# Weights in the program's layout, transposes inside the first product halves, and another order of the first queries

## The chip, the cores and the metric

One core of a Trainium2 chip runs the whole kernel. The metric is the device time of one execution in microseconds (us); lower is better. TensorE (PE) does matmuls and transposes, VectorE (DVE), ScalarE (ACT) and GpSimd (POOL) the elementwise work, SyncE (SP) and ACT issue the DMAs.

## The reference

The input is 4 sequences of 512 rows by 512 columns. The same macaron layer is applied: half a feed-forward block, an attention block, half a feed-forward block, each on a layer norm of the running sum.

```python
x = x + 0.5 * ffn(layernorm(x))       # y = x @ W_base.T + b, plus 4 gated rank-8 LoRA experts
x = x + attn(layernorm(x))            # 32 heads, latent keys and values of rank 64, causal
x = x + 0.5 * ffn(layernorm(x))       # same weights as the first

# ffn:   z = x @ A.T (4 experts x 8), alpha = softmax(log(prior) + x @ router.T + router_b)
#        y += sum_e alpha_e * 2 * z_e @ B_e.T
# attn:  c_q = x @ w_q_down (192), c_kv = x @ w_kv_down (64), k_rope = rope(x @ w_k_rope) (64)
#        q_lat = (c_q @ w_q_up_nope per head) @ w_uk per head, q_rope = rope(c_q @ w_q_up_rope)
#        probs = softmax((q_lat . c_kv + q_rope . k_rope) / sqrt(192), causal)
#        out = concat over heads((probs @ c_kv) @ w_uv.T) @ w_out
```

All is float32. The kernel splits each matmul operand into a high and a low part (names ending in `_hi` and `_lo`) and sums three products.

## The kernel before

The program is written engine by engine: every engine has its own in-order list of instructions, and semaphores tie the lists together. Nothing is planned at run time; the order in each list is the order in the code. It has these stages.

**Opening.** Weights are loaded and brought into the form that the matmuls need. `transpose_base` (L710 to L722) turns `W_base` with 16 PE transposes; `base_high` on ACT and `base_low` on DVE split the result. `transpose_lora` does the same for the small LoRA and router weights. Then the first feed-forward block runs on the 4 row tiles of sequence 0 (`s` = 4 to 7: `FIRST` is 4, `DOWN` is 8). One step of a tile on PE is: `ffn_products` half 0 (12 matmuls, 292 columns: half of the output, the LoRA `z` and the router logits), then `transpose_z` of the tile before, `transpose_x` of the tile after, `ffn_products` half 1 (12 matmuls, 256 columns), then `lora` of the tile before. Each transposed tile goes through ACT (`xT_high`) and DVE (`xT_low`) before the next products may use it. `gate_logits` and `gate_rows` on DVE, with `gate_exponentials` on ACT between, make the gated `z` (tile `za`) that `transpose_z` needs.

After that come the folds. `w_q_up_nope` is turned by `transpose_nope` (PE), copied out of PSUM by `nopeTa_copy` (ACT) and `nopeTb_copy` (DVE), and multiplied with `w_uk` in `fold_query` (8 groups of 4 heads); `query_hi` (ACT) and `query_lo` (DVE) split the product into the query weights. `fold_output` multiplies `w_uv` and `w_out` of a pair of heads (16 pairs); `output_hi` (ACT) and `output_lo` (DVE) split that. In the loop over the 8 groups, `fold_output` of group g - 1 follows `fold_query` of group g. The inputs of `fold_output` pass through 4 slots (`SLOTS_OUT`); SP refills a slot when PE has used it. The other 8 output folds lie between the down projections of the 4 row tiles (`s` = 8 to 11). The rotary query weights are split by ACT (`rotary_hi`) and POOL (three long subtractions with the down weights, L585, L589 and L592). POOL then makes the norms' rough deviations of the down tiles (`rough_deviations(2, ...)`).

`opening_queries` makes the queries of the first two heads in four parts: rows 0 to 383 of both heads (`EARLY`), then rows 384 to 511 of both (`LATE`). Each part goes PE, DVE (`q_rotary`), POOL (`q_sum`), ACT (`qT_high`), POOL (`qT_low`). The first score slot needs rows 384 to 511 of head 0.

**Attention** of a sequence: 80 slots, with scores, softmax, transposes, the product with the values, and output products, spread over all engines.

**Mixed steps**, between two attentions, three times: the second feed-forward block of sequence b (tiles 0 to 3), the first of sequence b + 1 (tiles 4 to 7) and its down projections (8 to 11), in the order 4, 5, 6, 7, 8, 0, 9, 1, 10, 11, 2, 3. On PE it is `steps` (L866); `down_products` has two halves of 6 matmuls. The norm of the next tile (`xn`) is made by ACT just ahead; for tile 8 it hangs on a chain of statistics on DVE, deviations on POOL and `norm` on ACT, and next to a down tile it is queued on ACT behind `down_copies`.

**Last steps**: the second feed-forward block of sequence 3 alone, tiles 0 to 3, and the stores.

## Time and profile before

| | us |
|---|---|
| median of 3 runs (lowest, highest) | 1167.78 (1166.98, 1170.35) |
| the profiled execution, its own time | 1167.57 |
| span of its instructions, first to last | 1165.8 |
| PE, DVE, POOL, ACT busy | 1105.7, 908.2, 740.0, 623.9 |
| opening, up to the first scores | 0 to 96.7 |
| the first mixed steps | about 319 to 370 |
| last feed-forward products to the end | 1142.8 to 1165.8 |

The profile is of one execution. Busy times are sums over an engine; matmuls overlap, so PE's busy time is an upper reading. All times below are from the start of the span. L with a number is a line of the kernel before.

### The profile page before, as it was taken

The page shows a single profiled execution, that of the slowest core. Times are in us where ns is not written, and L with a number is a line of the kernel's source. Part 1 is how long each engine was busy: PE and PEld are TensorE (multiplying, and loading weights), DVE is VectorE, ACT ScalarE, POOL GpSimd, SP SyncE. Part 2 cuts the span into 40 slices and gives each one's busy share as a digit, 9 for nine tenths or more (in the row PEclk, how much of TensorE's full clock was granted, in tenths as well). Part 3 has the DMA queues.
Part 4 walks back from the last instruction along what each step waited for, and adds up shares of the span by engine and source line. Part 5 has one row for each costly group of instructions (what it writes and reads, how often), then busy time and mean ns, then how long its engine had stood idle before and what let it go on. Part 6 is the DMA issues. An engine that isn't in the chain of part 4 may idle for free.

```text
span 1165.8 us, 21866 instructions
## 1 busy us (share of the span) xinstructions
PE 1105.7 (95%) x7284; PEld 906.6 (78%) x7284; DVE 908.2 (78%) x2667; ACT 623.9 (54%) x1733; POOL 740.0 (63%) x951
## 2 busy tenths in 40 slices
PE   5896999999998999999999899999999899999997
PEld 4755788888797788888788678888888678888876
DVE  4767888888676888878776888788867787888855
ACT  3554655555454655555535555655545466555542
POOL 2406977887432978787631887787723598877841
PEclk9998999999999999999999999999999999999998
DMA  9660000000101000000101000000010100000000
GB/s 286 179 194 1 1 1 1 1 1 1 37 10 64 2 1 2 1 1 1 37 1 37 37 2 1 2 1 2 1 37 28 47 1 1 1 1 2 1 1 37
DMA packets 22248, 30.96 MB, mean 27 GB/s; under 512 B 9302, under 2 KB 11094, under 8 KB 21498
## 3 DMA queue, kind: packets, MB, share of 16 engines
q1 hardware_dynamic: 19770, 24.85, 6.7%
q10 hardware_dynamic: 2368, 4.72, 1.2%
q8 instruction: 59, 0.97, 0.3%
q14 instruction: 51, 0.42, 0.1%
HBM read 22.23 MB, written 4.19 MB: 23 GB/s over the span
## 4 chain that ended last, share of the span: by engine, by line
PE 79%; DVE 7%; POOL 7%; ACT 3%; issue 2%; SPq 1%; DMA 1%; POOLq 0%; DVEq 0%
PE Y L983 15%; PE Y L957 12%; PE XZ L942 11%; PE Y L906 10%; PE XZ L922 6%; PE XZ L923 6%; PE XZ L921 5%; PE Y L675 4%; POOL prob L631 3%; PE XZ L675 2%; POOL qT_lo L542 2%; PE XZ L650 2%; POOL q_sums L537 2%; DVE xT_lo L1281 1%; ACT xT_hi L1037 1%
## 5 line engine op out<-in xcount | busy, mean ns | idle before, releaser
L1228 ACT ACTIVATE prob<-XZ,small 128x512 f32<-128x512 f32 (+3 forms) x512 | 266.3, 525 | 282.8 <-DVE small L1622 282.8
L631 POOL TENSOR_TENSOR prob<-prob,small 128x512 f32<-128x512 f32 (+3 forms) x512 | 360.7, 721 | 50.1 <-DVE small L1576 40.4
L1622 DVE CUSTOM_DVE_ANT_0 XZ<-XZ,mask 128x512 f32<-128x512 f32 (+3 forms) x512 | 247.9, 506 | 114.6 <-PE XZ L923 110.5
L537 POOL TENSOR_TENSOR q_sums<-q_sums,q_turned 64x512 f32<-64x512 f32 (+2 forms) x130 | 164.2, 1263 | 201.5 <-DVE q_turned L1564 200.1
L942 PE MATMUL XZ<-ident,prob 128*128 128x128 f32 x1280 | 196.3, 276 | 3.2 <-POOL prob L631 2.9
L921 PE MATMUL XZ<-kT_hi,qT_hi 128*128 128x512 f32 (+3 forms) x512 | 176.9, 345 | 12.7 <-ACT prob L1228 6.8
L542 POOL TENSOR_TENSOR qT_lo<-q_sums,qT_hi 128x512 fp32r<-128x512 f32 (+2 forms) x130 | 165.2, 1271 | 31.9 <-ACT qT_hi L1195 31.8
L942 PEld LDWEIGHTS XZ<-ident,prob 128*128 128x128 f32 x1280 | 149.5, 140 | 43.2 <-POOL prob L631 10.6
L922 PE MATMUL XZ<-kT_lo,qT_hi 128*128 128x512 f32 (+3 forms) x512 | 165.4, 323 | 0.0
L923 PE MATMUL XZ<-kT_hi,qT_lo 128*128 128x512 f32 (+3 forms) x512 | 165.2, 323 | 0.0
L957 PE MATMUL Y<-probT,ckv 128*64 128x384 f32 (+2 forms) x1280 | 152.3, 384 | 0.0
L390 ACT ACTIVATE probT<-XZ 128x512 f32<-128x512 f32 x192 | 114.9, 598 | 66.0 <-PE XZ L942 64.8
L957 PEld LDWEIGHTS Y<-probT,ckv 128*64 128x64 f32 x1280 | 81.8, 136 | 60.7 <-issue 47.3
L921 PEld LDWEIGHTS XZ<-kT_hi,qT_hi 128*128 128x128 f32 x512 | 97.2, 190 | 22.8 <-issue 7.7
L983 PE MATMUL Y<-wo_hi,oT_hi 128*128 128x512 f32 x256 | 110.9, 433 | 1.5 <-DVE x_sb L1580 1.4
L1580 DVE TENSOR_TENSOR x_sb<-Y,x_sb 128x512 f32<-128x512 f32 x128 | 87.8, 686 | 29.4 <-PE Y L983 29.1
L1228 ACT ACTIVATION_READ_ACCUMULATOR prob<-XZ,small 128x1 f32 x512 | 101.9, 199 | 0.0
L923 PEld LDWEIGHTS XZ<-kT_hi,qT_lo 128*128 128x128 f32 x512 | 97.3, 190 | 5.5
L922 PEld LDWEIGHTS XZ<-kT_lo,qT_hi 128*128 128x128 f32 x512 | 97.7, 191 | 4.8
L983 PE MATMUL Y<-wo_hi,oT_lo 128*128 128x512 f32 x256 | 101.1, 395 | 0.0
L983 PE MATMUL Y<-wo_lo,oT_hi 128*128 128x512 f32 x256 | 100.2, 391 | 0.0
L1195 ACT ACTIVATE qT_hi<-q_sums 128x512 fp32r<-128x512 f32 (+2 forms) x130 | 80.2, 617 | 19.0 <-POOL q_sums L537 19.0
(220 smaller groups left out, 2162.0 us busy)
## 6 DMA issues: line engine op xcount, KB each, us to landing
wout_nat<-in_L_attn_w_out_dram SPq DMA_DIRECT2D x16, 512.0 KB, 5.0
out_dram<-x_sb SPq DMA_DIRECT2D x16, 256.0 KB, 2.0
x_next<-_attn_hidden_states_dram SPq DMA_DIRECT2D x12, 256.0 KB, 3.4
x_sb<-x_next SPq DMA_DIRECT2D x12, 256.0 KB, 2.3
wbase_nat<-in_L_ffn_W_base_dram ACTq DMA_DIRECT2D x1, 1024.0 KB, 5.7
x_sb<-_attn_hidden_states_dram ACTq DMA_DIRECT2D x4, 256.0 KB, 7.0
nope_a<-_L_attn_w_q_up_nope_dram ACTq DMA_DIRECT2D x1, 1024.0 KB, 5.4
rope_a<-_L_attn_w_q_up_rope_dram SPq DMA_DIRECT2D x1, 1024.0 KB, 8.0
```

Of the source, the lines that this page charges most:

```text
L537: nc.gpsimd.tensor_tensor(q, q, turned, ALU.add).then_inc(q_sum_set, 1)
L542: nc.gpsimd.tensor_tensor(qT_lo[par][:, head, cols], q_sums[par][:, head, cols], f32(qT_hi[par][:, head, cols]), ALU.subtract).then_inc(qT ...
L631: last = nc.gpsimd.tensor_tensor(prob[u % RING][:, c:c + w], prob[u % RING][:, c:c + w], inv_sum[:, u % RING, m:m + 1].broadcast_to([P, w] ...
L906: last = nc.tensor.matmul(bank[:, cols], w, c, start=(j == 0), stop=(j == 4))
L921: nc.tensor.matmul(bank[:, c:c + w], high, kT_hi[:, 0:w], start=True, stop=False)
L922: nc.tensor.matmul(bank[:, c:c + w], high, kT_lo[:, 0:w], start=False, stop=False)
L923: last = nc.tensor.matmul(bank[:, c:c + w], low, kT_hi[:, 0:w], start=False, stop=True)
L942: last = nc.tensor.transpose(probT_ps[v % 2][:, at], prob[v % RING][:, at], ident[:])
L957: last = nc.tensor.matmul(o_ps[64 * h:64 * h + 64, column * P:(column + n) * P], ckv[:, j, :], probT[:, HEAD_BLOCKS * h + at:HEAD_BLOCKS * ...
L983: last = nc.tensor.matmul(bank, o[buffer][:, rows], w, start=(k == 0 and j == 0), stop=(k == 1 and j == 2))
L1228: last = nc.scalar.activation(prob[u % RING][:, c:c + w], score_ps[u % 2][:, c:c + w], ACT.Exp, bias=neg_max[:, u % RING, m:m + 1], scale= ...
L1622: last = nc.vector.tensor_tensor_reduce(bank, bank, mask[:, S - w:S], -1.0, HIGHEST, ALU.add, ALU.min, neg_max[:, u % RING, m:m + 1])
```

## The change

The host hands some weights over in another layout, so that PE need not turn `W_base` and `w_q_up_nope`, and so that the DMAs move long rows. `base_sb` is the turned base weight, in another place of SBUF, which is shared with the slots of `w_out`. ACT and DVE split it in two halves of 1024 columns, not in 8 pieces. The order of the loads on ACT's queue is now row tile 0, base weight, other row tiles, `w_uk`, first half of `w_q_up_nope`.

The eight query folds now follow each other, over four PSUM banks, and the first eight output folds follow behind them. The split of the down weights on ACT stands behind the fourth query fold. The gate's matmul (`spread_gates`) moves into the first products.

In all feed-forward and mixed steps, `transpose_z` and `transpose_x` move from the end of half 0 into its middle, and on DVE `z_low` and `xT_low` move ahead of `gate_logits`. The four query parts change order: head 0 rows 0 to 383, rows 384 to 511 of head 0 and head 1, then head 1 rows 0 to 383.

```diff
-                def ffn_products(b, s, half):
+                def ffn_products(b, s, half, inside=None):
                     a, z = ((0, W0), (W0, WB))[half]
                     for c in range(KC):
+                        if c == KC // 2 and inside:
+                            inside()
...
-                def down_products(b, s, half):
+                def down_products(b, s, half, inside=None):
                     for c in (2 * half, 2 * half + 1):
+                        if c == 1 and inside:
+                            inside()
...
+                def spread_gates():
+                    pe.wait_ge(turns_one, 1)
+                    pe.wait_ge(gate_in, 16 * 2 * NE)
+                    nc.tensor.matmul(gate_ps, cosT[0:1, 0:P], gate_row[:], start=True, stop=True).then_inc(gate_spread, 1)
...
                 def opening():                                   # PE
-                    transpose_base()
+                    pe.wait_ge(ident_set, 3)
                     transpose_x(-1, FIRST)
                     transpose_lora()
-                    pe.wait_ge(turns_one, 1)
-                    pe.wait_ge(gate_in, 16 * 2 * NE)
-                    nc.tensor.matmul(gate_ps, cosT[0:1, 0:P], gate_row[:], start=True, stop=True).then_inc(gate_spread, 1)
                     pe.wait_ge(lora_lo_set, 1)
+                    pe.wait_ge(base_hi, 2)
+                    pe.wait_ge(base_lo, 2)
...
-                        ffn_products(-1, s, 0)
-                        if s > FIRST:
-                            if s == FIRST + 1:
-                                pe.wait_ge(up_lo, 1)
-                            transpose_z(-1, s - 1)
-                        if s + 1 < DOWN:
-                            transpose_x(-1, s + 1)
+                        def transposes(s=s):
+                            if s == FIRST:
+                                spread_gates()
+                            else:
+                                if s == FIRST + 1:
+                                    pe.wait_ge(up_lo, 1)
+                                transpose_z(-1, s - 1)
+                            if s + 1 < DOWN:
+                                transpose_x(-1, s + 1)
+                        ffn_products(-1, s, 0, transposes)
                         ffn_products(-1, s, 1)
...
+                    transpose_z(-1, DOWN - 1)
+                    pe.wait_ge(nope_in[0], 16)
+                    pe.wait_ge(uk_in, 16)
                     pe.wait_ge(prior_set, 1)
-                    transpose_nope(0, 0)
-                    transpose_z(-1, DOWN - 1)
+                    pe.wait_ge(x_updated, ST - 1)
+                    for g in range(2):
+                        fold_query(g)
                     lora(-1, DOWN - 1)
...
+                    for g in range(2, G4):
+                        if g == G4 // 2:
+                            pe.wait_ge(nope_in[1], 16)
                         fold_query(g)
-                        if g:
-                            fold_output(g - 1)
-                    fold_output(G4 - 1)
+                    for i in range(PAIRS // 2):
+                        fold_output(i)
...
                     for i, s in enumerate(order):                # PE, steps
                         products = ffn_products if s < DOWN else down_products
                         wait_for_products(b, s)
-                        products(b, s, 0)
-                        if i and order[i - 1] < DOWN:
-                            transpose_z(b, order[i - 1])
-                        if i + 1 < len(order):
-                            transpose_x(b, order[i + 1])
+                        def transposes(i=i):
+                            if i and order[i - 1] < DOWN:
+                                transpose_z(b, order[i - 1])
+                            if i + 1 < len(order):
+                                transpose_x(b, order[i + 1])
+                        products(b, s, 0, transposes)
...
                 def opening_queries():                           # PE
-                    for j, (head, cols) in enumerate(FIRST_PARTS):
-                        if j == 2:
-                            transpose_down(-1, STEPS - 1)
-                            pe.wait_ge(ckT_hi, ST)
-                            pe.wait_ge(ckT_lo, ST)
-                        if j >= 2:
-                            pe.wait_ge(q_rot_set, j - 1)
-                        q_products(j, 0, head, qT_ps[head], cols)
+                    for head in range(2):
+                        q_products(0, 0, head, qT_ps[head], EARLY)
+                    transpose_down(-1, STEPS - 1)
+                    pe.wait_ge(ckT_hi, ST)
+                    pe.wait_ge(ckT_lo, ST)
+                    for head in range(2):
+                        q_products(0, 0, head, XZ[1][:, head, :], LATE)
...
                     for g in range(G4):                          # ACT, opening
-                        if g + 1 < G4:
-                            nopeTa_copy(g + 1, (g + 1) % 2)
                         query_hi(g)
-                        if g:
-                            output_hi(g - 1)
+                        if g == 3:
+                            act.wait_ge(down_in, 16)
+                            nc.scalar.activation(wd_hi[:], down_nat[:], ACT.Copy).then_inc(down_hi_set, 1)
+                    for i in range(G4 - 1):
+                        output_hi(i)
...
                     row_moments(FIRST).then_inc(var_set, 1)      # DVE, opening
+                    deviations(0, FIRST, 1, 1)
+                    norm(FIRST)
+                    base_low(0)
+                    fill_up()
+                    base_low(1)
                     for t in range(1, ST):
                         dve.wait_ge(x_in[t], 16)
                         nc.vector.bn_stats(stats[:, t, :], x_sb[:, t, :]).then_inc(stats_set, 1)
-                    deviations(0, FIRST, 1, 1)
-                    norm(FIRST)
...
-                        gate_logits(-1, s)
                         if s > FIRST:
                             z_low(-1, s - 1)
                         if s + 1 < DOWN:
                             xT_low(-1, s + 1)
+                        gate_logits(-1, s)
                         gate_rows(-1, s)
...
                     for g in range(G4):
-                        if g + 1 < G4:
-                            nopeTb_copy(g + 1, (g + 1) % 2)
                         query_lo(g)
+                        if g == 1:
+                            update_rows(-1, DOWN - 1)
                         if g:
-                            output_lo(g - 1)
-                        down_norms(g)
+                            down_norms(g - 1)
+                    down_norms(G4 - 1)
+                    for i in range(G4 - 1):
+                        output_lo(i)
...
+                        if i and ORDER[i - 1] < DOWN:            # DVE, mixed steps
+                            z_low(b, ORDER[i - 1])
+                        if i + 1 < MIXED:
+                            xT_low(b, ORDER[i + 1])
                         if s < DOWN:
                             gate_logits(b, s)
-                        if i and ORDER[i - 1] < DOWN:
-                            z_low(b, ORDER[i - 1])
                         if i == 3:
                             deviations(4 + 2 * b, 0, ST, GROUPS_0 + GROUPS * b + 3)
-                        if i + 1 < MIXED:
-                            xT_low(b, ORDER[i + 1])
```

## Rows read from the trace of the kernel before

**Rows 1.** Windows: stretch, its length, each engine's busy us, clock, DMA, GB/s.

```profile
43.90:65.20 21.30, 21.30 (x339) 13.71 (x337) 17.66 (x44) 13.63 (x30) 5.63 (x4) 1.00 0.51 146
319.12:362.21 43.09, 40.54 (x303) 38.10 (x302) 29.97 (x110) 21.54 (x61) 9.11 (x38) 1.00 0.07 26
1142.83:1165.80 22.97, 18.77 (x128) 18.10 (x128) 10.30 (x42) 6.34 (x18) 1.05 (x2) 0.87 0.12 46
```

**Rows 2.** Timeline of the opening: start, us, engine, line, operation, [idle before <-releaser].

```profile
10.35 0.40 SPq L459 DMA_DIRECT2D up_b<-in_L_ffn_lora_B_dram  x1
...
12.69 1.85 DVE L1417 BATCH_NORM_STATS2 stats<-x_sb 128x6 f32<-128x512 f32 x3
...
15.89 0.20 DVE L1358 COPY up_nat<-up_b 128x128 f32<-128x128 f32 x1
...
20.01 0.61 PE L675 MATMUL Y<-wb_hi,xT_hi 128*128 128x292 f32 x1
```

**Rows 3.** Chain that ended last, opening: start, us, what.

```profile
13.45 5.93 DMA gate_row<-_L_ffn_domain_prior_dram
```

**Rows 4.** Timeline, around the end of the opening's feed-forward block.

```profile
39.05 1.72 DVE L1297 TENSOR_SCALAR small<-small 128x4 f32<-128x4 f32 x1
```

**Rows 5.** Timeline of POOL in the opening.

```profile
36.16 4.59 POOL L585 TENSOR_TENSOR wq<-rope_bb,wq 64x2048 fp32r<-64x2048 f32 x1 [18.85 <-ACT wq L1073]
...
45.41 2.90 POOL L592 TENSOR_TENSOR wd_lo<-down_nat,wd_hi 128x1280 fp32r<-128x1280 f32 x1
```

**Rows 6.** DVE's groups, 43.9 to 65.2 us: names, shapes, xcount | busy us, mean ns | idle before.

```profile
L1372 DVE TENSOR_TENSOR wq<-Y,wq 64x256 fp32r<-64x256 f32 x8 | 3.4, 428 | 0.1
L1370 DVE TENSOR_TENSOR wq_lo<-Y,wq_hi 128x256 fp32r<-128x256 f32 x8 | 3.4, 422 | 3.0 <-ACT wq L1084 3.0
```

**Rows 7.** The page, part 6: DMA issues, KB each, median us to landing.

```profile
wout_nat<-in_L_attn_w_out_dram SPq DMA_DIRECT2D x16, 512.0 KB, 5.0
```

**Rows 8.** Chain that ended last, first queries to first attention.

```profile
92.44 1.01 POOL q_sums L537
...
95.21 0.46 POOL q_sums L537
...
96.74 0.77 PE XZ L921
...
102.83 1.28 POOL q_sums L537
```

**Rows 9.** What PE waited for, 319 to 363 us: total us, times, longest.

```profile
PE XZ L650 <- ACT xn L1163: 1.0, 3, 0.4
PE Y L675 <- DVE xT_lo L1281: 0.5, 2, 0.3
```

**Rows 10.** Chain that ended last, first mixed steps.

```profile
332.55 0.82 ACT xn L1163
...
333.41 0.66 PE XZ L650 x4
334.07 1.42 PE XZ L675 x12
...
338.90 1.85 PE Y L675 x12
340.74 0.45 PE XZ L650 x4
```

**Rows 11.** Timeline of DVE, first mixed steps.

```profile
335.90 0.29 DVE L1306 TENSOR_TENSOR za<-XZ,small 128x32 f32<-128x32 f32 x2
```

**Rows 12.** Chain that ended last, last steps.

```profile
1142.83 3.26 PE XZ L675 x12
1146.09 1.02 PE XZ L650 x4
1147.11 1.96 PE XZ L675 x12
```

**Rows 13.** Timeline of ACT, last steps.

```profile
1145.13 0.81 ACT L1163 ACTIVATE xn<-x_sb,shift,rstd 128x512 f32<-128x512 f32 x1 [3.49 <-DVE shift L1269]
```

More of the change, by code:

```diff
@@ L170, in build @@
         uk_sb = place("uk_sb", [P, H, KVL], F32, region_a)
-        nopeT_a = [place(f"nopeT_a{i}", [P, 4, P], F32, region_a) for i in range(2)]
-        nopeT_b = [place(f"nopeT_b{i}", [P, 4, 64], F32, region_a) for i in range(2)]
         assert region_a[0] <= region_b0
@@ L1097, in opening @@
                 def opening():
-                    act.dma_start(wbase_nat[:], W_base.rearrange("(c p) h -> p c h", p=P)).then_inc(ffn_in, 16)
-                    for t in range(ST):
+                    act.dma_start(x_sb[:, 0, :], hidden[0, 0:P, :]).then_inc(x_in[0], 16)
+                    act.dma_start(base_sb[:], base_T).then_inc(ffn_in, 16)
+                    for t in range(1, ST):
                         act.dma_start(x_sb[:, t, :], hidden[0, t * P:(t + 1) * P, :]).then_inc(x_in[t], 16)
-                    act.dma_start(uk_sb[:], w_uk.rearrange("(h d) r -> d h r", d=DN)).then_inc(uk_in, 16)
-                    for c in range(KC):
-                        base_high(c)
-                    act.dma_start(nope_a[:, 0:16, :], w_q_up_nope[0:P, 0:16 * DN]
-                                  .rearrange("q (h d) -> q h d", d=DN)).then_inc(nope_in[0], 16)
-                    act.dma_start(nope_b[:, 0:16, :], w_q_up_nope[P:QL, 0:16 * DN]
-                                  .rearrange("q (h d) -> q h d", d=DN)).then_inc(nope_in[0], 16)
+                    act.dma_start(uk_sb[:], uk_T).then_inc(uk_in, 16)
+                    act.dma_start(nope_sb[:, 0:16, :], nope_T[:, 0:16, :]).then_inc(nope_in[0], 16)
+                    act.wait_ge(consts_set, 1)
+                    nc.scalar.activation(warm_slot[:, 0:1], three_halves[0:1, :], ACT.Ln)
+                    base_high(0)
                     xT_high(-1, FIRST)
+                    base_high(1)
                     act.wait_ge(loraT_ps, 1)
@@ L1423, in opening @@
                     last.then_inc(var_set, 1)
-                    fill_up()
                     xT_low(-1, FIRST)
@@ L1658, with at @@
     nc = _bacc.Bacc("TRN2", target_bir_lowering=False, num_devices=1, dynamic_dma_scratch_size=4096)
+    def at(name):
+        return _np.asarray(inputs[name])
     arrays, args = {}, []
-    for name in _INS:
-        a = _np.ascontiguousarray(inputs[name])
+    down = _np.concatenate([at("L0_attn_w_q_down"), at("L0_attn_w_kv_down"), at("L0_attn_w_k_rope")], axis=1)
+    laid = {
+        "hidden": at("L0_attn_hidden_states"),
+        "w_down": down.reshape(KC, P, DC).transpose(1, 0, 2),
+        "nope_T": at("L0_attn_w_q_up_nope").reshape(QL, H, DN).transpose(2, 1, 0),
+        "w_q_up_rope": at("L0_attn_w_q_up_rope"),
+        "uk_T": at("L0_attn_w_uk").reshape(H, DN, KVL).transpose(1, 0, 2),
+        "uv": at("L0_attn_w_uv").reshape(PAIRS, 2, DV, KVL).transpose(0, 2, 1, 3),
+        "w_out": at("L0_attn_w_out").reshape(PAIRS, 2, DV, D).transpose(0, 2, 1, 3),
+        "base_T": at("L0_ffn_W_base").T.reshape(KC, P, D).transpose(1, 0, 2),
+        "bias": at("L0_ffn_b_base").reshape(KC, P).T,
+        "lora_A": at("L0_ffn_lora_A"),
+        "lora_B": at("L0_ffn_lora_B").reshape(-1, KC, P, R).transpose(0, 2, 1, 3),
+        "router_W": at("L0_ffn_router_W"),
+        "router_b": at("L0_ffn_router_b"),
+        "domain_prior": at("L0_ffn_domain_prior"),
+        "active": at("L0_ffn_active"),
+    }
+    for name, a in laid.items():
+        a = _np.ascontiguousarray(a)
         arrays[f"in_{name}_dram"] = a
```

165 lines of the change are left out of this document (53 added, 112 removed).

## The prediction

> **What bounds the kernel now.** I first read the windows, stage by stage [rows 1]. In the mixed steps PE is busy for 40.54 of 43.09 us and in the opening's folds for all of 21.30: the reader is to see that the folds have PE work to lose, and that the mixed steps have little idle time that an earlier transpose could win back. Then the waits of PE in the mixed steps [rows 9]: 1.0 us in 3 waits for `xn`, the normed tile that a transpose reads, and only 0.5 us in 2 waits for `xT_lo`, the product of a transpose. So in this stage the input of the transposes is late, not their output. Last the chain of waits through the opening and the first queries [rows 3, 8], where POOL links the pieces.
>
> **The first feed-forward block.** The 16 base transposes and their splits go. What remains ahead of the first products, which start at 20.01 in before [rows 2], is DVE's list: `fill_up` waits for the LoRA loads, and behind it stand the second half of `base_low` (1024 columns; an estimate of 1.2 us, from 0.42 us for 256 [rows 6], at most four times that), three row statistics (1.85 [rows 2]) then the moments, `xT_low` and the LoRA split (an estimate of 1.4: 656 columns at 0.42 for 256, and small change), with 0.5 for `fill_up` itself. The loads land somewhere between their last issue at 10.75 and 15.89, when `fill_up` runs [rows 2]. I take 14.3, past the middle, because the gate's DMA in the same queue took 5.93 us [rows 3]. That puts the products at 19.25, 0.75 earlier (bounds 3 earlier, 1.5 later).
>
> The Trainium skill speaks against part of this ("DMA: Bandwidth & Descriptors", "Queues, rings and completion order"): a DMA engine takes turns between queues, a packet at a time. ACT's queue now holds the rows of `w_uk` and `w_q_up_nope` as long pieces while SP's small LoRA loads pass; by this rule they land later, and the first products would start at the late bound, some 2 us behind my figure. The long wait of the gate's DMA agrees with the rule; no run here shows the new order.
>
> Little of this reaches the folds. The last tile's gating waits in DVE: its L1297 took 1.72 us and ended at 40.77, with POOL's first rotary subtraction, 36.16 to 40.75 [rows 4, 5]. That subtraction starts when ACT has split the rotary weights behind tile 6's gate, and that gate now stands behind `xT_low`. I take tile 7's `z` to be transposed 0.2 us earlier (bounds 1.9 earlier, if the stall goes, to 1.0 later).
>
> **The folds.** Of PE's 21.30 us the nope transposes go, and of DVE's 17.66 seven PSUM copies [rows 1]. But the order is serial now. DVE must first do eight `query_lo` of two instructions, 0.42 and 0.43 us, with gaps 0.88 a group, 7.0 us [rows 6]; between them stand the last row update, four statistics, the moments, four small deviations and two norms, an estimate of 5.6 us (17.66 less 7 copies of 0.42, the 6.8 of `query_lo` and seven output splits of some 0.65 leaves 3.4; the overlaps of 44 instructions, some 1.5, and the update, 0.65, come on top). A stall comes to it: the deviations need POOL, and POOL's down-weight subtraction (2.90 [rows 5]) now waits for a split on ACT behind the fourth query fold, at about 48; it ends at 50.9, the rough deviations at 52.3, 0.7 us after DVE asks. With the first fold at 41.7, behind the transposed `z` and a row update, and 1.7 us for it and ACT, DVE starts its first output split at 56.7. The eight output folds then go through two PSUM banks: fold, ACT, DVE, back to PE, about 2.35 us for two, so the last leaves PE at 63.8. Their inputs hold them a little more: slots 2 and 3 are free at 58.5 and 59.4, and a refill takes 5.0 us to land behind 0.4 of issue [rows 7], so folds 6 and 7 run to 65. The first down transposes start at 65.20 in before, the end of that window. I take 0.1 earlier (bounds 1.2 earlier, with quick refills, to 2.5 later), so the folds' 6 us of PE work buy nothing. The term for all up to the down tiles is -0.3. The down tiles' own steps are as before.
>
> **The first queries.** Before the first score PE waits for three parts, two of them long. A long part is one link of POOL and ACT from 92.44 to 95.21, 2.77 us [rows 8]. Now only one long part and one short one stand ahead, so the scores begin 2.77 us before 96.74. The second long part runs behind the two short ones, and POOL is through with it at 98.05, as early as in before; the next pair's sum, at 102.83 in before [rows 8], comes at about 100.1, so it hides. Taken: -2.8 (bounds -3.2 to -1.0, the latter if POOL holds up the second pair).
>
> **The mixed steps, three times.** PE's work does not change; the transposes move forward by half of half 0, 0.8 to 0.9 us (half of 1.85 [rows 10]). A transpose whose `xn` is ready does not care, and its ACT and DVE work gains that time. One whose `xn` came just in time stalls PE with these 0.9 us still undone.
> - Tiles 4, 5 and 6: `xn` is early; each step is bound by PE's own work, 0.1 us a step is won at the start, 0.3 together.
> - Tile 7: the `xn` of tile 8 is done at 333.37 [rows 10], by DVE, POOL and ACT, none of which starts earlier. The transposes stay at 333.4, and 0.9 us of products follow that preceded them: 0.9 less 0.3 is +0.6.
> - Tile 8: DVE now has the gate of tile 7 behind `xT_low` of tile 8, and five small deviations (1.0 us) behind both. The `za` that ended at 336.19 [rows 11] ends at about 337.25; PE wants it at 336.9. The next step, at 338.90 in before [rows 10], starts 0.85 late.
> - Tile 0: the `xn` of tile 9 follows the down copies, and was there just ahead of 340.74 [rows 10]. It moves with the 0.85 and now finds PE waiting in the middle: +1.5.
> - The later steps take turns. A step next to a down tile stalls for `xn`, the following one runs faster, since the `xT_lo` waits (0.5 [rows 9]) are gone: 0.3 comes back.
>
> That is +1.25 a stage (bounds -1.1, the waits of [rows 9] with those for keys, to +2.5), +3.75 for three.
>
> **The last steps.** PE starts at 1142.83 at half clock: 12 matmuls in 3.26 us [rows 12], against 1.85 later [rows 10]. `xn` of the second tile is done at 1145.94 [rows 13], just ahead of the transposes at 1146.09. In the middle of half 0, at 1144.4, PE would stall for 1.6 us; the clock may rise during the rest (12 matmuls took 1.96 [rows 12]). The lost 1.6 less 0.65, for products that would fall behind the clock's rise, is 0.95; if the stall holds the clock down for longer, 2.6. I take +1.3.
>
> **The sum.** -0.3 - 2.8 + 3.75 + 1.3 = +1.95 on the profiled 1167.57 (span 1165.8 and 1.77 around it), which is 0.2 below the median: 1169.5 us.
>
> **Rivals.**
> - *The earlier transposes pay.* If `xn` and `za` are in time after all (DVE reordered frees ACT and the norms), the mixed steps lose their waits, 1.1 us each, and the last steps stay: -0.3 - 2.8 - 3.3 = -6.4: 1161.2. For it: 0.5 us of waits for `xT_lo` [rows 9]. Against: 1.0 us for `xn`, and 94% of the stage is PE's work.
> - *The folds shrink with their work.* PE's window is full [rows 1] and loses 6 to 7 us of transposes. If output folds overlapped query folds, 6 us would go, and with my other terms it is 1163.5. Against: the lists of PE and DVE put all output work behind.
> - *The gate becomes the bound* (slower). With logits behind `xT_low`, ACT's exponential, an estimate of 0.45 us there and back, is covered by nothing on DVE. Once `za` comes later than the middle of the next half 0, each of the 7 gated steps pays it: 3.2 a stage, 9.6 in all instead of 3.75: 1175.4. It decides where DVE has more to do in a step than PE's 4.2 us (1.85, 0.45, 1.42 [rows 10] and the LoRA products); in tiles 6 and 7, with row updates and statistics, it is near that. Against: later steps have room.
> - *The folds end late* (slower). Refills of 7 us and a clock that drops while PE waits for `za` put the down tiles 2.5 us back instead of 0.3 ahead: 1172.3.
>
> **Chances.** Forecast 0.45; transposes pay 0.16; folds shrink 0.09; gate 0.14; folds late 0.16. About 0.3%, 3.5 us, can be told from no change: under 1164.3 or over 1171.3. The two fast cases are faster, 0.25; the two slow ones slower, 0.30, and 0.03 of the forecast's own spread: faster 0.25, same 0.42, slower 0.33. The forecast's own range is 1166 to 1172; with the rivals 1162.5 to 1174.5.
>
> **What would show it.** First scores at 93 to 94.5, against 96.74. First down transposes within 1.5 us of 65.2, with PE idle between query and output folds. In the mixed steps PE waits for `xn` inside half 0, more than 3 us a stage, and none for `xT_lo`; the stage from the first products to the first query products over 44 us, against 43.09. In the last steps a PE wait of 1.6 us at about the fifth to seventh matmul. A mixed stage under 42.5 us would make the forecast wrong, as would down transposes before 62.

## The result, and the profile after

The changed kernel takes 1183.56 us (median of 4 runs, 1182.85 to 1184.42) against 1168.07 beside it: 1.013 times as long, 95% interval 1.0113 to 1.0148. The forecast was 1169.5, range 1162.5 to 1174.5. The profiled execution took 1184.42 us, span 1182.64; before 1167.57 and 1165.78. The ledger below accounts for these 16.9 us of span; the medians are 15.5 us apart.

Cut at the same events, the two traces give a ledger. The events are PE's first feed-forward products, the last tile's z transposed, the first down products, the first score, and in each batch the last score, the first products and the first query products.

| stretch | before | after | forecast | measured |
|---|---|---|---|---|
| up to first products | 20.01 | 21.49 | -0.75 | +1.48 |
| four tiles, up to z of the last | 21.22 | 22.50 | +0.55 | +1.28 |
| folds, up to first down products | 26.20 | 31.28 | -0.1 | +5.08 |
| down tiles, first queries, first score | 29.31 | 27.12 | -2.8 | -2.19 |
| three mixed stages | 129.27 | 135.70 | +3.75 | +6.43 |
| four attentions, first to last score | 828.52 | 831.49 | 0 | +2.97 |
| last steps | 22.95 | 24.66 | +1.3 | +1.71 |

The forecast's first three cells are its -0.3, split by its own times (19.25 for the first products, z 0.2 earlier, 0.3 ahead at the down tiles). The rows sum to +16.76; the last 0.1 lies in the gaps between the events.

The first two rows hold some of what differs between traces of the same code. Two kernels below leave before's opening as it is: their first products start at 20.97 and 20.38 instead of 20.01, and their tiles take 21.59 us each instead of 21.22. Three leave the changed kernel's opening as it is up to `z`: 21.32, 21.30 and 21.23, and 22.49 each. So the first row is worth +0.3 to +1.5, the second +0.9 to +1.3.

The windows of the changed kernel, with the columns of [rows 1] (stretch, length, busy us by engine, granted clock, DMA share, GB/s): the four tiles, the folds, down tiles and queries, the first mixed stage, the last steps.

```profile
21.49:43.99 22.50, 18.71 (x126) 17.22 (x126) 12.75 (x43) 9.37 (x19) 5.30 (x3) 1.00 0.74 251
43.99:75.27 31.28, 22.50 (x302) 12.77 (x302) 18.93 (x42) 11.74 (x27) 8.29 (x4) 0.80 0.39 139
75.27:102.39 27.12, 22.36 (x122) 14.57 (x121) 17.47 (x48) 11.76 (x33) 2.96 (x5) 0.94 0.33 112
324.77:369.94 45.17, 40.55 (x303) 37.71 (x302) 30.26 (x110) 22.57 (x61) 9.27 (x38) 1.00 0.06 24
1157.98:1182.60 24.62, 18.70 (x128) 17.93 (x128) 10.40 (x42) 6.70 (x18) 1.05 (x2) 0.86 0.11 43
```

The first row of [rows 1] starts later and ends 2.2 us earlier than the second one here. The same stretch of before, as a window:

```profile
41.23:67.43 26.20, 24.76 (x358) 15.76 (x358) 21.39 (x50) 16.99 (x36) 8.30 (x4) 1.00 0.48 141
```

PE has 56 matmul records fewer now, and the stretch is 5 us longer: PE is idle for 8.8 us of it instead of 1.4, and its clock is down to 0.80. The clock is at its lower level in three stretches of it: in the query folds, from PE's wait for DVE into the output folds, and at the last output fold.

```profile
45.80:49.20 3.40, 3.40 (x49) 3.06 (x47) 1.78 (x5) 1.32 (x4) 2.39 (x1) 0.51 0.02 5
59.40:66.20 6.80, 3.66 (x10) 1.07 (x12) 4.16 (x8) 0.60 (x1) 0.00 (x0) 0.50 0.30 94
73.10:75.27 2.17, 2.01 (x6) 0.30 (x5) 1.35 (x2) 0.74 (x2) 0.00 (x0) 0.50 1.04 403
```

In the mixed stage PE is busy for 40.55 us, as before (40.54), and idle for 4.62 instead of 2.55.

The opening's timeline, as in [rows 2] (start, us, engine, line):

```profile
16.88 0.23 DVE L1321 COPY up_nat<-up_b 128x128 f32<-128x128 f32 x1 [8.01 <-DMA up_b<-in_lora_B_dram]
...
17.30 1.22 DVE L1314 TENSOR_TENSOR wb_lo<-base_sb,wb_hi 128x1024 fp32r<-128x1024 f32 x1
...
18.43 1.87 DVE L1377 BATCH_NORM_STATS2 stats<-x_sb 128x6 f32<-128x512 f32 x3
...
21.49 0.61 PE L656 MATMUL Y<-wb_hi,xT_hi 128*128 128x292 f32 x1 [2.92 <-DVE wb_lo L1384]
```

DVE stands idle for 8 us until the LoRA load is in, at 16.88, and does the second half of the base split and the statistics of three tiles only then.

The end of the feed-forward block, as in [rows 4, 5]:

```profile
38.92 4.59 POOL L564 TENSOR_TENSOR wq<-rope_bb,wq 64x2048 fp32r<-64x2048 f32 x1 [17.05 <-ACT wq L1045]
...
41.59 1.95 DVE L1261 TENSOR_SCALAR small<-small 128x4 f32<-128x4 f32 x1
...
43.99 0.33 PE L674 MATMUL XZ<-ident,za 128*128 128x128 f32 x1 [1.56 <-DVE za L1270]
```

DVE's four-column instruction again ends with POOL's subtraction (43.51), not after its own 0.23 us, and PE waits 1.56 us for it.

The chain of waits through the folds (start, us, what):

```profile
51.62 1.17 ACT wd_hi L1097
...
52.86 2.91 POOL wd_lo L571
...
56.01 1.03 POOL rough L490
57.05 0.17 DVE newton L1224
...
61.70 0.70 DVE wo_lo L1354
...
62.54 4.66 PE XZ L740 x12
67.21 0.33 SPq L424
...
67.58 5.74 DMA wout_nat<-in_w_out_dram
...
73.36 1.98 PE Y L740 x4
```

ACT splits the down weights late, POOL subtracts late, DVE gets its rough deviations at 57.05 and comes to the first output split at 61.70, five us after the forecast's 56.7; PE's output folds free a slot only then, and the slot's refill ends the chain. PE's waits in this stretch name the split and the refill (total us, times, longest):

```profile
PE XZ L740 <- DVE wo_lo L1354: 6.1, 2, 5.5
PE XZ L740 <- DMA wout_nat<-in_w_out_dram: 1.8, 1, 1.8
```

The first queries, as in [rows 8]: only two POOL sums stand ahead of the first score now. From the first query products to that score it takes 7.25 us (95.14 to 102.39) instead of 10.02 (86.72 to 96.74), 2.77 less.

```profile
98.09 1.00 POOL q_sums L516
...
100.86 0.46 POOL q_sums L516
...
102.39 0.76 PE XZ L892
```

PE's waits in the first mixed stage, as in [rows 9]:

```profile
PE XZ L629 <- ACT xn L1127: 3.8, 5, 1.2
PE XZ L674 <- DVE za L1270: 0.8, 3, 0.4
```

The waits for `xT_lo` are gone; those for `xn` rose from 1.0 to 3.8. The chain at the fourth step shows one, as in [rows 10]: POOL's deviations, `xn`, then the transposes.

```profile
337.84 0.20 POOL shift L510
338.07 0.82 ACT xn L1127
338.89 0.04 issue
338.94 0.67 PE XZ L629 x4
```

The last steps, as in [rows 12, 13]: `xn` ends 3.13 us after the first products, as before (3.11), and 18 matmuls, not 12, stand behind it. PE stands idle for it for 1.80 us, from 1159.36.

```profile
1160.29 0.82 ACT xn L1127
1161.11 0.04 issue
1161.15 1.12 PE XZ L629 x4
1162.27 3.65 PE XZ L656 x18
```

### The profile page after: what moved, and what is told of

The parts are those of the page before. It is cut to its first block, busy times and chain, and to the rows that moved or that the text cites. A ratio compares the mean times of both kernels' runs of the same rounds, so it can differ in the third digit from the quotient of the medians.

```text
span 1182.6 us, 21665 instructions
## 1 busy us (share of the span) xinstructions
PE 1103.0 (93%) x7204; PEld 900.4 (76%) x7204; DVE 906.2 (77%) x2653; ACT 620.7 (52%) x1718; POOL 741.3 (63%) x951
## 4 chain that ended last, share of the span: by engine, by line
PE 75%; DVE 10%; POOL 7%; ACT 4%; issue 2%; DMA 2%; SPq 1%; POOLq 0%; DVEq 0%
PE Y L954 15%; PE Y L928 12%; PE XZ L913 11%; PE Y L874 10%; PE XZ L893 6%; PE XZ L894 6%; PE XZ L892 5%; PE Y L656 3%; POOL prob L610 3%; PE XZ L629 2%; POOL q_sums L516 2%; POOL qT_lo L521 2%; PE XZ L656 1%; ACT xn L1127 1%; DVE xT_lo L1245 1%
## 5 line engine op out<-in xcount | busy, mean ns | idle before, releaser
L516 POOL TENSOR_TENSOR q_sums<-q_sums,q_turned 64x512 f32<-64x512 f32 (+1 forms) x130 | 164.4, 1264 | 211.3 <-DVE q_turned L1521 210.0
L521 POOL TENSOR_TENSOR qT_lo<-q_sums,qT_hi 128x512 fp32r<-128x512 f32 (+1 forms) x130 | 165.6, 1274 | 31.8 <-ACT qT_hi L1159 31.3
L1159 ACT ACTIVATE qT_hi<-q_sums 128x512 fp32r<-128x512 f32 (+1 forms) x130 | 80.3, 618 | 18.0 <-POOL q_sums L516 18.0
## 6 DMA issues: line engine op xcount, KB each, us to landing
nope_sb<-in_nope_T_dram ACTq DMA_DIRECT2D x1, 1536.0 KB, 11.2
```

The lines of the kernel that those rows point to most:

```text
L516: nc.gpsimd.tensor_tensor(q, q, turned, ALU.add).then_inc(q_sum_set, 1)
L521: nc.gpsimd.tensor_tensor(qT_lo[par][:, head, cols], q_sums[par][:, head, cols], f32(qT_hi[par][:, head, cols]), ALU.subtract).then_inc(qT ...
```

## The experiments

**The steps.** Three kernels separate PE's order, DVE's order, and z from x.

`steps_old`: the changed kernel with the old steps.

```diff
-                        products(b, s, 0, transposes)
+                        products(b, s, 0)
+                        transposes()
...
+                        if s < DOWN:
+                            gate_logits(b, s)
                         if i and ORDER[i - 1] < DOWN:
                             z_low(b, ORDER[i - 1])
```

> The changed kernel with the mixed and the last steps as they were: transposes behind half 0 on PE, gate logits ahead of the splits on DVE. Between first products and first query products the changed kernel's three mixed stages are 2.0 to 2.3 us longer than before, its last steps 1.7, and its second and third attention 2.0 and 1.0. Theory A (the moved transposes and splits cost 8.1 us in the steps, and the attention's half clock follows from PE's added idle time): stages of 43.1, attention 206.9 each, 1183.6 - 11.1 = 1172.5. Rival B (the half clock in attention has nothing to do with the steps): stages of 43.1, one or two attentions stay longer, 1175.5. Rival C (the longer stages come from the new layout or the clock, not from the order): stages of 45, 1183. First scores at 102.4 in all.

Measured: 1173.2 us (6 runs), 1.0046 of before (1.0032 to 1.006). Mixed stages 43.12, 43.10, 43.09. First scores at 101.3. The attentions take 207.1, 207.9, 206.9, 206.9. Theory A holds for the steps, C falls. One attention stays 1 us longer with the old steps, as B said, so A's second half is not shown. The first scores were expected at 102.4 and come 1.1 us earlier, with nothing edited ahead of them.

`before_inside`: the kernel before, with PE's move alone.

```diff
-                        products(b, s, 0)
-                        if i and order[i - 1] < DOWN:
-                            transpose_z(b, order[i - 1])
-                        if i + 1 < len(order):
-                            transpose_x(b, order[i + 1])
...
+                        products(b, s, 0, transposes)
```

> The kernel before, with PE's transposes of the mixed and last steps moved into the middle of half 0 and nothing else; DVE's order stays. Theory A (PE stalls in mid half for a normed tile that comes at its old time, as the prediction had it): mixed stages 44.3 to 45.3 instead of 43.1, last steps +1.3 to 1.7, 1168.1 + 5 to 8 = 1173 to 1176. Rival D (it is DVE's order, the gate behind the splits, that costs): stages within 0.4 of 43.1, 1168 to 1169.5.

Measured: 1178.14 us (6 runs), 1.0081 (1.0066 to 1.0096). Stages 45.20, 45.14, 45.13; last steps 25.3 instead of 22.95. D falls: PE's move alone gives the whole length of the changed kernel's stages (45.17 the first), and beside it the new order on DVE changes nothing. The time is above A's 1173 to 1176: the steps explain 8.5 us, and the first scores, 1.35 us later than before's, and the attentions, 1.0 us longer together, lie where nothing was edited. PE's waits in its first stage:

```profile
PE XZ L650 <- ACT xn L1170: 4.2, 5, 1.2
PE Y L688 <- DVE xT_lo L1288: 0.3, 1, 0.3
PE XZ L695 <- DVE za L1313: 0.2, 1, 0.2
```

`z_inside`: the kernel before, with only z transposed inside.

```diff
+                        products(b, s, 0, transposes)
+                        if i + 1 < len(order):
+                            transpose_x(b, order[i + 1])
```

Here `transposes` holds `transpose_z` alone.

> The kernel before, with PE's transpose of the gated z alone moved into the middle of half 0 of the mixed and last steps; the four transposes of the next tile stay behind half 0. Theory K (PE stalls for the normed next tile, xn): mixed stages of 42.8 to 43.4 against 43.1, last steps as before. Theory L (PE stalls for the gate's za): mixed stages of 44.5 to 45.2.

Measured: stages 43.86, 43.84, 43.85; last steps 22.35; 1170.23 in one run. That is between the two: z takes 0.76 of the 2.06 us, which leaves 1.3 to x. K is right on the larger part, and the gate's `za` is late too, by half a microsecond at one step (neither theory put the stages there):

```profile
PE XZ L650 <- ACT xn L1170: 0.9, 3, 0.4
PE XZ L695 <- DVE za L1313: 0.5, 1, 0.5
```

**The opening.** Five kernels, each the changed one with one part of its opening undone.

`loads_fill`: the nope load is issued later, and DVE copies the LoRA weights later.

```diff
-                    act.dma_start(nope_sb[:, 0:16, :], nope_T[:, 0:16, :]).then_inc(nope_in[0], 16)
                     base_high(1)
+                    act.dma_start(nope_sb[:, 0:16, :], nope_T[:, 0:16, :]).then_inc(nope_in[0], 16)
...
-                    fill_up()
                     base_low(1)
...
                     xT_low(-1, FIRST)
+                    fill_up()
```

> The changed kernel with two edits in its opening: ACT issues the load of the first half of the nope weights behind the second base split instead of at 3.8, and DVE copies the LoRA weights behind the second base split, the statistics and the first x split instead of ahead of them. Theory G (large loads of one queue hold back small ones of the other): the last LoRA load lands at 14.0 to 14.8 instead of 16.85, first products at 15.5 to 16.5 instead of 21.5, and 4 to 5.5 us arrive at the first scores: 1178 to 1179.5. Rival H (the LoRA loads land when they are issued, at 16.9 whatever else is loaded): first products at 18 to 18.6, 1180 to 1181. Rival I (the last tile's gate or the folds take it back): first products early, first scores at 101 or later, 1182 to 1184.

Measured: 1177.18 us (6 runs), 1.0085 (1.0068 to 1.0101). First products at 17.92, first scores at 97.57, 4.8 earlier. The gain at the scores is in G's range, but 1.1 of it lies in the folds and the down tiles, where nothing was edited. The landing and the first products are H's: the LoRA loads are in only at 16.51. The nope load, issued at 8.04 and landed at 16.19, still ran beside them, so this run does not tell G from H.

`load_only`: the nope load behind the LoRA split, and nothing else.

```diff
                                          ACT.Copy).then_inc(lora_hi_set, 1)
+                    act.dma_start(nope_sb[:, 0:16, :], nope_T[:, 0:16, :]).then_inc(nope_in[0], 16)
```

> The changed kernel with one edit: ACT issues the load of the first half of the nope weights behind the split of the LoRA weights instead of at 3.8 us. In the changed kernel the last LoRA load landed at 16.85 and the last of the gate's small loads at 18.29. Theory G (a large load in ACT's queue holds back the small loads in SP's queue while both run): LoRA loads complete at 13.8 to 14.3, first products at 18.5 to 19.3 instead of 21.5, and the gate's loads, now beside the nope load, complete at 18.5 to 19.5. Rival H (LoRA loads end when SP has issued them, the other queue does not matter): complete at 16.5 to 16.9, first products at 21.2 to 21.5.

Measured: the LoRA loads are in at 13.95, first products at 18.59, the gate's loads at 19.40 instead of 18.29; 1176.42 in one run. G, with all its numbers; H falls. Of the 5.8 us at the first scores (96.64), 2.9 are there at the first products; most of the rest lies in the folds, at another clock (below). DVE's first LoRA copy, to be read against 16.88 above:

```profile
13.98 0.23 DVE L1321 COPY up_nat<-up_b 128x128 f32<-128x128 f32 x1 [5.13 <-DMA up_b<-in_lora_B_dram]
```

`ffn_old`: the four tiles in their old order.

```diff
-                        ffn_products(-1, s, 0, transposes)
+                        if s == FIRST:
+                            spread_gates()
+                        ffn_products(-1, s, 0)
+                        transposes()
...
+                        gate_logits(-1, s)
                         if s > FIRST:
                             z_low(-1, s - 1)
```

> The changed kernel, the four feed-forward tiles of its opening as before: transposes behind half 0, gate logits ahead of the splits, the gate's bias spread ahead of the first products. From the first products to the transposed z of the last tile the changed kernel takes 22.50 us, the one before 21.22. Theory M (the transposes in mid half cost it): 21.0 to 21.5, and 1 us of it at the first scores (101.4). Rival N (the table load on ACT or the loads cost it): 22.2 to 22.6, first scores at 102.4.

Measured: 20.77 us from first products to z instead of 22.50, first scores at 98.20, not 101.4; 1177.90 in one run. M on the tiles, with 1.7 us, for its three edits together: the transposes, the gate's place on DVE and the gate's matmul. Another 2.3 us are in the folds, where nothing was edited (windows: the tiles, the folds):

```profile
21.89:42.66 20.77, 17.79 (x124) 17.00 (x124) 12.34 (x42) 9.14 (x19) 4.93 (x2) 1.00 0.79 264
42.66:71.62 28.96, 20.24 (x301) 11.30 (x301) 18.93 (x42) 11.80 (x27) 8.29 (x4) 0.94 0.39 134
```

PE is busy for 20.24 us there instead of 22.50: the clock is 0.94 of full instead of 0.80. `load_only`, with the folds unedited too, has 28.99 us at 0.94.

`split_early`: the down weights split ahead of the query folds.

```diff
                     z_high(-1, DOWN - 1)
+                    act.wait_ge(down_in, 16)
+                    nc.scalar.activation(wd_hi[:], down_nat[:], ACT.Copy).then_inc(down_hi_set, 1)
                     for g in range(G4):
                         query_hi(g)
-                        if g == 3:
-                            act.wait_ge(down_in, 16)
-                            nc.scalar.activation(wd_hi[:], down_nat[:], ACT.Copy).then_inc(down_hi_set, 1)
```

> The changed kernel with one edit: ACT splits the down weights ahead of the query folds instead of behind the fourth; output folds stay behind all query folds. Theory E (the order costs, the late split only its own stall): DVE's wait for the rough deviations, 55.3 to 57.05, goes, the first output split starts at 59.8 to 60.4 instead of 61.7 and the first down products at 73 to 74 instead of 75.3. Rival O (the late split is the whole loss of the folds): first down products at 66 to 68.

Measured: first output split at 59.45, first down products at 72.09, first scores at 98.67; 1179.25 in one run. More than E said, far less than O. The folds take 28.37 us at clock 0.94, so against the two kernels above the early split is worth 0.6 us; the rest goes with the clock.

`woven`: `split_early`, and output fold g-2 behind query fold g on three engines.

```diff
                         fold_query(g)
-                    for i in range(PAIRS // 2):
+                        fold_output(g - 2)
+                    for i in range(G4 - 2, G4):
                         fold_output(i)
```

> The changed kernel with output fold g-2 behind query fold g on PE, ACT and DVE, and the split of the down weights on ACT ahead of the query folds, as before; only the query folds' transposes stay away. Theory E (the folds' gain was lost in their order: DVE reaches the first output split only at 61.7, and the slots' refills start late): first down products at 65 to 67 instead of 75.3, first scores at 92.5 to 94.5 instead of 102.4, 1183.6 - 8 to - 10 = 1173.5 to 1175.5. Rival F (DVE and the loads of the output slots set the time whatever the order): first down products at 72 to 74, 1181 to 1182.

Measured: 1173.66 us (6 runs), 1.0046 (1.0033 to 1.006); first down products at 65.61, first scores at 92.16. E, and F falls. The folds' window, z to first down products:

```profile
43.79:65.61 21.82, 18.18 (x302) 11.49 (x302) 18.13 (x42) 12.59 (x28) 8.29 (x4) 1.00 0.57 188
```

It is the same 302 matmul records as in the changed kernel, in 9.5 us less, and 4.4 us less than in before with its 358. Against `split_early`, which also splits early, the weaving is worth 6.5 us; the clock stays full, so what it costs in the serial order is in that figure. PE's wait for a slot's load is gone, and that for `wo_lo` fell from 6.1 to 2.0.

**A version that beats both.** `best` takes the new layout and queries, and undoes what lost; the transposes stay inside half 0 only for the first three tiles of a mixed stage.

```diff
+                        products(b, s, 0, transposes if i < 3 and not alone(b) else None)
+                        if i >= 3 or alone(b):
+                            transposes()
...
                     pool.wait_ge(rope_hi_set, 1)
+                    pool.wait_ge(alpha_set, ST)
```

> The changed layout with what the runs so far point to: woven folds with the early down split, mixed and last steps in the old order but for the transposes of the three tiles whose input is early (inside half 0), LoRA weights copied late, the nope load issued behind the LoRA split, the opening's later tiles in the old order, and POOL's rotary subtractions behind the last tile's alpha. Theory (the losses are separate and add up: folds 10.2, loads 4.8 and 1.5 more by the later nope load, opening steps 1.3, alpha's stall 1.9, mixed steps 0.3 a stage gained over before): first products at 15.5 to 16.5, first scores at 83 to 86 against 96.74 before, stages of 42.8, 1153 to 1158 against 1167.8. Rival (the folds then wait for the loads of the output weights, which land at 34 to 40, or POOL's late subtractions hold the output splits): first scores at 88 to 90, 1159 to 1162.

Measured: 1159.63 us (6 runs), 0.9926 (0.9911 to 0.9941). First products at 15.47, mixed stages 42.64, 42.59, 42.66 (0.45 less than before). First scores only at 88.74, where the rival put them, and by its second reason in part: POOL's later subtraction kept DVE's first output split from 45.9 to 47.45. The rest neither theory had: the nope load, now at 14.8, held the gate's small loads to 19.47, and PE waited for them from 17.3 to 19.6 in the first tile.

`best2` mends these two: the gate is spread behind half 0 of the first tile, the second tile's transposes ahead of it, the nope load issued beside the exponential's table load, and POOL's first subtraction is cut in two around the last tile's alpha.

```diff
+                    nc.gpsimd.tensor_tensor(wq2[64:P, 0:16, KVL:HD], rope_bb[64:P, 0:16, :],
+                                            f32(wq2[64:P, 0:16, KVL:HD]), ALU.subtract)
                     pool.wait_ge(alpha_set, ST)
-                    nc.gpsimd.tensor_tensor(wq2[64:P, :, KVL:HD], rope_bb[64:P, :, :], f32(wq2[64:P, :, KVL:HD]),
-                                            ALU.subtract).then_inc(rope_lo_set, 1)
+                    nc.gpsimd.tensor_tensor(wq2[64:P, 16:32, KVL:HD], rope_bb[64:P, 16:32, :],
+                                            f32(wq2[64:P, 16:32, KVL:HD]), ALU.subtract).then_inc(rope_lo_set, 1)
...
+                        if s == FIRST:
+                            spread_gates()
+                        else:
                             transposes()
```

> The previous best kernel with its opening taken on: the second tile's transposes and splits ahead of the gate's bias, which is spread behind half 0 of the first tile; the nope load behind the table load for the exponential; and POOL's first rotary subtraction in two halves, the second behind the last tile's alpha. Theory (the gate's chain of loads, logarithm and table load stood ahead of the second tile): second tile's products at 20 to 21 instead of 24.68, the last tile's z transposed at 34.5 to 36 instead of 38.56, first scores at 84 to 86 instead of 88.74, 1154 to 1157. Rival (the weights' loads or the gate's exponential then hold the tiles or the folds): z at 37 to 38.5, first scores at 87.5 to 89, 1158 to 1160.

Measured: 1155.11 us (4 runs), 0.9884 (0.9861 to 0.9907). Second tile at 20.61, z at 34.99, first scores at 83.71: the theory, with the scores 0.3 earlier than it put them. Its windows: four tiles, folds, down tiles with queries, first mixed stage.

```profile
15.25:34.99 19.74, 18.02 (x128) 17.01 (x126) 10.75 (x42) 8.95 (x20) 2.86 (x2) 1.00 0.94 329
34.99:57.15 22.16, 18.12 (x303) 11.36 (x302) 18.34 (x42) 13.25 (x29) 10.55 (x5) 1.00 0.78 276
57.15:83.71 26.56, 21.79 (x121) 14.02 (x121) 17.48 (x48) 11.24 (x33) 2.96 (x5) 0.99 0.37 123
306.09:348.68 42.59, 40.14 (x304) 37.97 (x302) 29.71 (x110) 21.78 (x61) 9.11 (x38) 1.00 0.07 26
```

Alpha takes its 0.23 us again, between POOL's halves:

```profile
31.31 2.38 POOL L564 TENSOR_TENSOR wq<-rope_bb,wq 64x1024 fp32r<-64x1024 f32 x1 [17.11 <-ACT wq L1053]
...
34.21 0.23 DVE L1270 TENSOR_SCALAR small<-small 128x4 f32<-128x4 f32 x1
34.51 2.39 POOL L567 TENSOR_TENSOR wq<-rope_bb,wq 64x1024 fp32r<-64x1024 f32 x1 [0.81 <-DVE small L1270]
```

## Why the prediction was wrong

**The step that failed** is "I take 0.1 earlier (bounds 1.2 earlier, with quick refills, to 2.5 later), so the folds' 6 us of PE work buy nothing." That the order eats the gain was right; that it ends there was not. The first down products came 7.8 us later than before, 8.1 later than forecast. PE stood idle for 5.5 us behind the first two output folds, where the prediction had named idle time ahead of all of them as the sign. The loads and tiles ahead make 3.0 of the 8.1 and the folds 5.2, twice this step's late bound:

- *The loads, 2.2 us.* "I take 14.3, past the middle" for the LoRA loads: they came at 16.85. With the nope load out of the way they came at 13.95, and the products 2.9 us earlier. In before's trace the same loads were in at 14.40 (the last count of their semaphore), so the figure was before's time; it had no term for the nope load, now issued at 3.8 instead of 11.2. The Trainium skill's rule ("DMA: Bandwidth & Descriptors", "Queues, rings and completion order": a DMA engine takes turns between queues, a packet at a time) was weighed and priced at some 2 us behind my figure; the products came 2.24 behind it. The trace agrees with that rule, and `load_only` with it.
- *The tiles, 0.7 us beside the forecast (1.3 beside before).* The prediction followed the loads and the last tile's gate, and gave no price to the transposes in mid half of the opening's own tiles. They are the same edit as in the mixed steps. Here PE stands for tile 4's `za` in the middle of tile 5's half 0, from 28.38 to 28.87; undoing them, with the gate's two moves, gave 1.7 us.
- *Half clock in the folds, some 2.3 us.* PE was granted 0.80 of its clock there, against 0.94 in `load_only` and `ffn_old` with the same folds and 1.00 in before. The first of its three stretches puts 1.5 us ahead of ACT's split (44.68 to 51.62 from the first query fold, 6.9 us; 5.5 in `load_only`), the third 0.9 into the last output fold (1.98 us; 1.08 in `load_only`). The prediction had the clock in a rival and not in this sum. `steps_old` and `loads_fill` have the first stretch too, `load_only`, `ffn_old` and `split_early` do not, with the same folds; why stays open.
- *The late split and the refills, the other 2.9 us.* DVE's stall for the rough deviations was foreseen at 0.7 us and is 1.76 (55.29 to 57.05), since ACT's split began at 51.6, not 48; by `split_early` the late split is worth 0.6 us at equal clock. The rest goes with the order: refills wait for folds that wait for DVE. PE waits 5.5 us for DVE's first output split, and the folds behind that wait run at half clock, the second stretch (`load_only` has one there too, 58.1 to 61.5). So slots 2 and 3 are free 2.8 and 4.6 us after that split begins, against 1.8 and 2.7 in the forecast, and the last refill takes 5.74 us, against 5.0. No run has the serial order at full clock, so the order's share and the clock's are not told apart.

"The folds shrink with their work" had a chance of 0.09 and its mechanism stands: with output folds between query folds the folds take 21.82 us instead of before's 26.20. It was the order that the change chose, not the work, that forbade it. "The folds end late" had the right sign and the right two reasons in kind (refills, clock), with a price of 2.5 us where 7.8 came, 5.1 of them in the folds.

**The first queries**: right. -2.77 between first query products and first score by the trace, -2.8 forecast; the down tiles ahead of them gave 0.58 back.

**The mixed steps**: right mechanism, half the size, 2.14 a stage instead of 1.25. Set against the stage's start, the first stage's steps lie 0.26, 0.16 and 0.32 us ahead of before's at tiles 5, 6 and 7 (forecast 0.3), +0.67 behind at tile 8 (+0.6), +0.72 at tile 0 (+0.85), +1.41 at tile 9 (+1.5). So far the term is right. "0.3 comes back" is what failed: the later steps lost 0.66 more, most of it at the last one. There tile 3's `xn` stands behind the down copies of the step just ended; it comes 2.2 us after PE starts the next products (before 2.1), the transposes were 0.25 us early for it behind half 0 and are 1.2 early in mid half. Waits for `xn` of "more than 3 us a stage, and none for `xT_lo`", as the prediction had it, are what the rows show (3.8 and none). That DVE's gate behind `xT_low` makes `za` late at tile 8 is not what happened: `before_inside`, with DVE's old order, has the first stage's steps at the same times within 0.2 us. Nor does the gate become the bound: PE's waits for `za` are 0.8 us in the stage.

**The last steps**: +1.71 against +1.3, with the stall where it was put, of 1.80 us against 1.6. The clock moves this row too: `steps_old`, with before's order there, takes 22.34 us against before's 22.95, with half clock from 1147.1 to 1150.5 where before has it from 1141.4 to 1148.2.

**Attention**: +3.0, forecast at nothing. Two attentions had a stretch at half clock some us after their start: 2.0 and 1.0 us longer. In the changed kernel's second attention, windows of the stretch ahead and the stretch itself:

```profile
386.00:390.40 4.40, 2.06 (x15) 1.52 (x14) 3.79 (x12) 1.38 (x8) 3.89 (x4) 1.00 0.00 0
390.40:394.00 3.60, 3.44 (x8) 2.70 (x9) 1.53 (x5) 2.71 (x9) 3.16 (x6) 0.53 0.00 0
```

PE was busy for 2.06 of 4.40 us and then had 8 matmul records in 3.60 us at the lower of its two levels (0.53 on the average). The moved transposes are not its cause, or not alone: every kernel here has one to three of its four attentions 0.4 to 2.2 us longer than the rest, with the old steps too (before 0.8, `steps_old` 1.0, `best2` 1.7 and 1.0). Why it takes one start and not the next stays open; no run here was made for it.

**Its arithmetic**: three sums do not close, and none is what failed. The transposes "0.1 earlier" stand beside a term of -0.3 for all up to the down tiles. The mixed steps' parts give 1.5 less 0.3, +1.2 and not +1.25. The waits of [rows 9] add to 1.5 us, not to the 1.1 of the first rival.

## What to carry to other kernels

Moving an instruction ahead on the engine that bounds a stage pays only as far as its input is early: list each step's input against the place it is moved to, and move those with slack (the moves at the first three tiles gain 0.45 us a stage here; all of them lose 2.1). Work taken off a full engine was worth nothing here until the orders on the other engines let it close up; keep producer and consumer woven (6.5 us against `split_early`, 9.5 against the changed kernel), above all where the consumer passes through few buffers. And here a large early load in one queue delayed the small loads that the first product waits for, so issue it when these are in.

## What the runs showed of the hardware

- A 1.5 MB load on ACT's queue put the end of SP's small LoRA loads from 13.95 (`load_only`) to 16.85; moved to 14.7, it put the gate's from 18.29 to 19.40 instead; issued after both, in `best2`, they end at 13.84 and 16.23.
- DVE's four-column TENSOR_SCALAR took 1.95 us beside a POOL subtraction and 0.23 between two. The Trainium skill has it ("SBUF — State Buffer", "Who interferes with whom": of DVE and GpSimd, the one that issues first has their shared port pair for its whole instruction, and the other is blocked; `tensor_scalar` is among the DVE instructions that can take the pair). The trace agrees: it ended 0.03 us behind POOL's. With POOL's instruction cut in two around it, in `best2`, PE's wait of 1.56 us for `za` at that place is gone.
- The same folds took 31.28 us at a mean clock of 0.80 and 28.96 at 0.94, in kernels that differ only ahead of them. PE is busy for 2.26 us more and the stretch is 2.3 longer: though PE is idle for 8.8 us of it, the loss came through whole, since the chain of waits runs through the folds that were slow.
